# Products by C in the selective scan: five on VectorE with states left in PSUM, eleven on GpSimd

## The reference

```
xn    = rmsnorm(x) * norm_w
xp, z = split(xn @ Win)                       # 256 channels each
xc    = silu(causal_conv4(xp) + conv_b)
dt, B, C = split(xc @ Wx)                     # 64, 16, 16
delta = softplus(dt @ Wdt + bdt)
h[t]  = exp(delta[t] * A) * h[t-1] + (delta[t] * xc[t]) * B[t]     # 256 channels x 16 states
y[t]  = sum over states of h[t] * C[t]  +  xc[t] * Dp
x     = x + (y * silu(z)) @ Wblk
```

## Time and profile before

| | us |
|---|---|
| timed runs, median of 3 (lowest, highest) | 2146.39 (2145.01, 2146.58) |
| profiled execution, span from first to last instruction | 2143.5 |

### The profile page before, as it was taken

The page is one execution under the profiler, slowest core; times in us unless marked ns, Lnnn a source line. Parts: engine busy times, 40 slices in busy tenths (PEclk is TensorE's granted clock), DMA queues, the critical chain, the costliest instruction groups (busy, mean ns, idle before and its releaser), DMA issues.

```text
span 2143.5 us, 34659 instructions
## 1 busy us (share of the span) xinstructions
PE 1877.8 (88%) x10816; PEld 1183.1 (55%) x10816; DVE 1943.2 (91%) x1826; ACT 1683.8 (79%) x3053; POOL 1458.1 (68%) x1364
## 2 busy tenths in 40 slices
PE   4788888888888888888888888888888799999998
PEld 1444444444444444444444445444444499989998
DVE  3799999999999999999999999999999987767775
ACT  4899999899999998989999999999999433333333
POOL 2688888888888888888888988888889600000000
PEclk9899999999999999999999999999999999999999
DMA  7323232323232323232333333332322200000000
GB/s 241 86 64 79 63 78 62 78 62 78 62 79 63 80 65 79 64 79 65 81 78 73 81 76 79 78 78 62 78 62 72 84 1 11 11 12 11 11 6 11
DMA packets 72786, 138.55 MB, mean 65 GB/s; under 512 B 13072, under 2 KB 31120, under 8 KB 68112
## 3 DMA queue, kind: packets, MB, share of 16 engines
q1 hardware_dynamic: 66320, 119.28, 22.7%
q10 hardware_dynamic: 6400, 18.42, 3.7%
HBM read 63.85 MB, written 7.74 MB: 33 GB/s over the span
## 4 chain that ended last, share of the span: by engine, by line
ACT 27%; PE 26%; POOL 26%; issue 13%; DVE 6%; ACTq 1%; SPq 1%; DMA 1%; POOLq 0%; DVEq 0%
POOL scan L478 12%; POOL scan L472 11%; PE y_ps L1291 11%; ACT decay L563 10%; PE dbu_ps L1266 8%; ACT scan L641 6%; DVE scan L829 3%; POOL scan L469 2%; PE dbu_ps L1067 2%; ACT sp_e L600 2%; ACT delta L601 2%; ACT sp_l L610 2%; PE y_ps L1052 2%; ACT sp_e L605 1%; ACT du_t L626 1%
## 5 line engine op out<-in xcount | busy, mean ns | idle before, releaser
L829 DVE TENSOR_TENSOR_SCAN scan<-decay,dbu_ps 128x1024 f32<-128x1024 f32 x512 | 1154.6, 2274 | 29.8 <-PE dbu_ps L1067 21.9
L1067 PE MATMUL dbu_ps<-ident,scan 128*128 128x128 f32 x4096 | 571.6, 286 | 220.7 <-DVE scan L829 195.9
L478 POOL TENSOR_TENSOR scan<-scan,c_rep 128x1024 f32<-128x1024 f32 x255 | 671.8, 2635 | 130.4 <-ACT du_t L626 66.5
L1067 PEld LDWEIGHTS dbu_ps<-ident,scan 128*128 128x128 f32 x4096 | 482.2, 147 | 500.1 <-DVE scan L829 259.3
L563 ACT ACTIVATE decay<-d_rep,a_cur 128x510 f32<-128x510 f32 x1024 | 668.0, 709 | 54.1 <-POOL scan L478 15.7
L472 POOL TENSOR_SCALAR scan<-du_t,b_t 128x256 f32<-128x256 f32 x896 | 594.8, 679 | 0.0
L641 ACT ACTIVATE scan<-du_t,b_t 128x256 f32<-128x256 f32 x1024 | 445.6, 494 | 1.2
L838 DVE TENSOR_TENSOR scan<-scan,c_rep 128x1024 f32<-128x1024 f32 x257 | 331.0, 1288 | 0.0
L766 ACT ACTIVATE decay<-dbu_ps 128x512 f32<-128x512 f32 x256 | 147.9, 597 | 205.2 <-PE dbu_ps L1266 183.1
L1052 PE MATMUL y_ps<-scan,sel 128*32 128x512 f32 x2048 | 299.8, 661 | 0.0
L1080 PE MATMUL pre_ps<-xn,w_pre 128*128 128x512 f32 x512 | 245.5, 603 | 5.2 <-DVE w_pre L818 5.2
(11 more groups left out here) (110 smaller groups left out, 1648.8 us busy)
## 6 DMA issues: line engine op xcount, KB each, us to landing
d_rep<-delta SPq DMA_DIRECT2D x496, 128.0 KB, 2.9
c_rep<-c_rows SPq DMA_DIRECT2D x32, 1024.0 KB
w_pre<-prepared_weights ACTq DMA_DIRECT2D x15, 866.0 KB, 13.0
prepared_weights<-scan SPq DMA_DIRECT2D x3, 1122.0 KB, 12.9
scan<-in_conv_w SPq DMA_DIRECT2D x4, 512.0 KB, 5.0
w_out<-prepared_weights SPq DMA_DIRECT2D x16, 128.0 KB, 12.5
sp_e<-in_x_rows SPq DMA_DIRECT2D x8, 256.0 KB, 3.2
d_rep<-in_w ACTq DMA_DIRECT2D x2, 1024.0 KB, 6.8
```

The costliest lines, as they stand in the source:

```text
L478: nc.gpsimd.tensor_tensor(ring[slot % RING], ring[slot % RING], c_rep[par][:, slot // PRS, :].unsqueeze(1).broadcast_to([128, 2, TG]), ALU ...
L829: nc.vector.tensor_tensor_scan(ring[slot % RING].rearrange("p u t -> p (u t)"), decay[slot % DEC].rearrange("p u a t -> p (u a t)"), dbu_p ...
L1067: last = nc.tensor.transpose(dbu_ps[slot % 2][:, u, 128 * j:128 * j + 128], dbu_t[m % 2][:, j, b, :, :].rearrange("p q c -> p (q c)"), ide ...
```

## The change

Six things are changed together.

1. Five of a step's 16 products by C (slots 0, 4, 8, 12, 14) are made on DVE and eleven on POOL; before it was eight and eight. In the five slots the scan writes its states back into `dbu_ps`, and the product reads them there and writes the `ring`. The product follows its own scan directly (before, it followed the next slot's scan). PE may refill that `dbu_ps` tile only when the product is done.
2. The bias bdt becomes row 96 of the weights of `project_dt`, and a row of ones is added to `dbc`. The Relu parts of softplus go from ACT; the two Abs become one of 1024 elements over both banks; DVE's last sum reads max(dt, 0) straight from PSUM.
3. `silus` is cut in two: x in slot 3 ahead of that slot's `outer`, z in slot 4 behind that slot's `exps`.
4. `turn_b` and `copy_bt` come ahead of `project_dt` (slots 5 and 6), whose two matmuls now wait for `root` (slot 7); Abs, Exp, Square and Ln follow each other in slot 8.
5. `project_out` uses the bank `y_ps[1]`, in slot 8, and `copy_out` follows the logarithm in slot 8; the second `skip` matmul waits for that copy.
6. Conv taps, `quad`, `turn_du`, `outer` shares and `normalise` move by a slot or so; an `outer` share that is empty no longer waits.

The diff, cut to its core:

```diff
+DVE_SLOTS = (0, 4, 8, 12, 14)
-SHARE = (0, 2, 5, 8)
+SHARE = (0, 3, 5, 8)
-POOL_SHARE = (0, 2, 3, 4, 4)
-POOL_FIRST = (0, 0, 2, 3, 4)
+POOL_SHARE = (0, 2, 2, 4, 4)
+POOL_FIRST = (0, 1, 3, 4, 4)
+UPPER_TAPS = (0, 3, 4)
+LOWER_TAPS = (0, 1, 3, 4)
 ...
+                sp.dma_start(pre[l][NBC:NBC + 1, W_DT:W_DT + DI].rearrange("a (k p) -> a k p", k=KT),
+                             bdt[l:l + 1, :, :].rearrange("a p k -> a k p"),
 ...
             def outer(s, par, m, first, last):
-                if first == 0:
+                if first == 0 and last:
 ...
-            def softplus_parts(s):
-                    nc.scalar.activation(sp_e[:, k, :], bank, ACT.Abs, bias=bias)
-                    nc.scalar.activation(delta[:, k, :], bank, ACT.Relu, bias=bias).then_inc(dt_used, 1)
+            def softplus_abs(s):
+                act.wait_ge(dt_ready, 2 * s + 2)
+                nc.scalar.activation(sp_e[:, :, :], pre_all[:, :, :], ACT.Abs).then_inc(act_sp, 1)
+                act.wait_ge(act_sp, 2 * s + 1)
+                nc.scalar.activation(sp_e[:, :, :], sp_e[:, :, :], ACT.Exp, scale=-1.0).then_inc(act_sp, 1)
 ...
+                    if slot == 3 and has(s, 1):
+                        silu_x(s + 1, nxt)
                     if has(s, 0) and m < M and p:
                         outer(s, par, m, SHARE[p - 1], SHARE[p])
-                    if slot == 3 and has(s, 1):
-                        silus(s + 1, nxt)
+                    if slot == 4 and has(s, 1):
+                        silu_z(s + 1)
 ...
             def scan(s, slot):
+                states = dbu_ps[slot % 2][:, :, :] if by_vector(s, slot) else ring[slot % RING]
-                nc.vector.tensor_tensor_scan(ring[slot % RING].rearrange("p u t -> p (u t)"),
+                nc.vector.tensor_tensor_scan(states.rearrange("p u t -> p (u t)"),
 ...
-                nc.vector.tensor_tensor(ring[slot % RING], ring[slot % RING],
+                nc.vector.tensor_tensor(ring[slot % RING], dbu_ps[slot % 2][:, :, :],
 ...
-                            nc.vector.tensor_tensor(delta[:, :, :], delta[:, :, :], sp_l[:, :, :], ALU.add)\
+                            nc.vector.scalar_tensor_tensor(out=delta[:, :, :], in0=pre_all[:, :, :], scalar=0.0,
+                                                           in1=sp_l[:, :, :], op0=ALU.max, op1=ALU.add)\
 ...
-            def project_dt(s):
-                pe.wait_ge(dbc_ready, s + 1)
+            def project_dt(s, k):
+                if k == 0:
+                    pe.wait_ge(bt_ready, s + 1)
+                elif has(s, 1):
+                    pe.wait_ge(ln_done, s + 2)
```

More of the change, by code:

```diff
@@ L58 @@
 W_CB = W_DT + DI
-W_DB = W_CB + KT
-W_D = W_DB + KT
+W_D = W_CB + KT
 W_PRE = W_D + DI
@@ L304, in is_last, with by_vector, vector_products, pool_products @@
             return has(s, 0) and not has(s, 1)
+        def by_vector(s, slot):
+            return slot in DVE_SLOTS or is_last(s) and slot == SLOTS - 1
+        def vector_products(s, slot):
+            return DVE_C * s + sum(by_vector(s, n) for n in range(slot + 1))
+        def pool_products(s, slot):
+            return POOL_C * s + sum(not by_vector(s, n) for n in range(slot + 1))
         def has(s, offset):
@@ L1062, in to_channels @@
                     pe.wait_ge(dbut_act, ACT_OUTER * (M * s + m + 1))
-                wait(pe, scan_done, SLOTS * s + slot - 1)
+                back, before = (s, slot - 2) if slot >= 2 else (s - 1, slot - 2 + SLOTS)
+                if has(s, -1) or slot >= 2:
+                    if by_vector(back, before):
+                        pe.wait_ge(hc_dve, vector_products(back, before))
+                    else:
+                        pe.wait_ge(scan_done, SLOTS * back + before + 1)
                 for u in range(2):
@@ L1138, in turn_du @@
                 pe.wait_ge(du_ready, s + 1)
-                pe.wait_ge(bt_ready, s + 1)
-                wait(pe, x_ready, s - 1 + X0 if has(s, -2) else 0)
                 for h in range(2):
@@ new lines, in window @@
+                    if slot == 5 and has(s, 1):
+                        turn_b(s + 1)
+                    if slot == 7 and has(s, 1):
+                        project_dt(s + 1, 1)
+                        project_dt(s + 1, 0)
+                    if slot == 8 and has(s, 0):
+                        skip(s, i, par, 1)
+                    if slot == 6 and has(s, 0):
+                        quad(s, 0, 0)
+                    if slot == 9 and has(s, 0):
+                        quad(s, 0, 1)
+                    if slot >= 9 and slot % 2 and has(s, 0):
+                        quad(s, (slot - 5) // PRS, (slot - 5) % PRS // 2)
```

176 lines of the change are left out of this document (83 added, 93 removed).

## The result

The changed kernel takes 2169.6 us (median of 2164.7 to 2186.4), the kernel before took 2145.7 beside it: ratio 1.0141, 95% interval 1.0114 to 1.0167. It is slower, where 2136 and "faster" were forecast. The profiled execution is the fastest of the four: 2164.69 us, span 2162.9.

The account below looks back on a forecast made before the run. ACT was taken to lead, DVE following closely. ACT's terms sum to -0.28 us per window (51.2), -8.4 over some 30; with -4 and +1.5 at the ends, span 2132.6, plus 2.9 for the median: 2136 us, range 2106 to 2174.

Parts of the forecast that it names:

- terms 1 to 3: ACT per window: z wait goes -2.29, dbc wait -0.24; softplus with one Abs -1.19; two more table loads +2.84 us.
- The start: Passed once: new dt wait and `turn_b` ahead of dt about +1, bdt loads +0.5 us.
- Term 4: ACT at the Abs: new wait for dt, which now follows `root`, +0.45 us per window if PE stands ready.
- term 5: ACT's wait for the DMA of delta into `d_rep`, now paid in full: 0 to 0.33, taken +0.15 us per window.
- Term 2: ACT's softplus: one Abs of 1024 elements handing over to Exp replaces four parts, -1.19 us per window.
- the relief of products: POOL's products fall from 2.635 towards the undisturbed 2.36 us; eight give 2.2 us back per window.
- the tail's -4: Last window, where ACT waits for DVE: fewer DVE products save 5 us, taken as -4.
- Of the rivals the second: Hand-overs between ACT and PE from dbc copy to Abs replace the z wait; slower, about 2167 us; chance 0.27.

Follow-up runs that it names:

- e9: Kernel before the change, with one more wait on SP so the load of C is issued later in each window: 2148.3 us, ratio 1.0035.
- e2: Changed kernel with the reload of `w_pre` cut to the bias columns, so that part of the work is left out: 2141.4 us, ratio 0.9991.
- e7: Changed kernel with the copy of dbc, and so the store and load of C, moved to slot 4 straight behind the z silus: 2159.4 us, ratio 1.0084.
- e1: Changed kernel with POOL's normalisation moved back from slot 6 to slot 7, behind the product of slot 6: 2154.8 us, ratio 1.0061.
- e10: Changed kernel with the edits of e1 and e2 together, normalisation later and no full reload of `w_pre`: 2109.1 us, ratio 0.9843.
- e8: Changed kernel with z silus behind slot 3's copies, C's copy in slot 4, reload ahead of Abs, normalisation later: 2114.5 us, ratio 0.9858.

## Why the prediction was wrong

**What held.** ACT's terms 1 to 3 came nearly as priced: the z and dbc waits are gone, and ACT is busy 48.6 us per window (1118.40 in 23.0), where the terms make 47.3 - 1.19 + 2.84 = 49.0. ACT's table loads, answering to the earlier trace rows:

```profile
798.02 1.29 ACT L658 ACTIVATE scan<-du_t,b_t 128x256 f32<-128x256 f32 x3
799.33 1.28 ACT L583 ACT_TABLE_LOAD   x1
800.63 1.33 ACT L583 ACTIVATE decay<-d_rep,a_cur 128x510 f32<-128x510 f32 x2
801.98 1.28 ACT L601 ACT_TABLE_LOAD   x1
803.27 1.08 ACT L601 ACTIVATE sz<-pre_ps 128x512 f32 x2
```

It is 1.31 us from end to start at a load, with no drain. A scan into PSUM (second row, 2277 ns in the mean) costs what one into SBUF does:

```profile
L850 DVE TENSOR_TENSOR_SCAN scan<-decay,dbu_ps 128x1024 f32<-128x1024 f32 x351 | 789.7, 2274 | 29.5 <-PE dbu_ps L1094 20.1
L850 DVE TENSOR_TENSOR_SCAN dbu_ps<-decay,dbu_ps 128x1024 f32<-128x1024 f32 x161 | 366.6, 2277 | 86.4 <-PE dbu_ps L1094 86.3
```

POOL's products take 2367 ns. POOL was relieved by more than assumed, 44.3 us per window instead of 49, as its `outer` products fell too, from 679 to 480 ns. The undisturbed windows, 50.6 to 51.1, come near the forecast's 51.2, though DVE's softplus is held in them too. The start cost +1.5, as said; its two parts were not measured apart. Term 4 was 0.19 instead of 0.45.

**What failed: term 5**, "paid in full: between 0 and 0.33, I take +0.15". ACT's wait for the broadcast rose from 0.33 to 1.04 us per window (23.9 / 23.0), +0.71. Its bound was wrong, since it took the landing as fixed. It rightly said that such a wait is now paid in full: in the kernel before, a window with a wait of 3.2 us takes 53.1 where its neighbours take 51.5, as its z wait is 1.0 instead of 2.55; in the changed kernel one with a wait of 5.0 takes 55.7 where the undisturbed ones of its kind take 50.6. But the landing moved, by 2.3 us. Term 2's own gain (1.19 us) brings the logarithm, and the reload behind it, nearer to the load of C: C's store lay 13.29 us ahead of the logarithm's end and lies 12.06 ahead. e9 makes most of this shift alone, 1.0 us, and the landing follows by 1.6; e2 and e7 show that it goes with how the three transfers lie. The remaining 0.7 us are within the scatter of the means. delta's 2 us have no share that e1 could show.

**What had no term: the softplus on DVE.** The prediction saw that POOL and DVE disturb each other and credited the relief of products. It took DVE's softplus to stay as it was, three instructions in 3.8 us, without a row for the new order. It did not ask which instructions with two SBUF inputs remain on DVE and what POOL now issues beside them. The first of the three took, before and after (min/median/max ns):

```profile
L860 DVE SCALAR_TENSOR_TENSOR sp_w<-sp_w,sp_e x32: 1204/1240/1480, 38.3 to 1632.7; 128x1024 f32<-128x1024 f32 x32
L882 DVE SCALAR_TENSOR_TENSOR sp_w<-sp_w,sp_e x32: 1224/3385/3406, 39.7 to 1651.6; 128x1024 f32<-128x1024 f32 x32
```

It is over 3 us in 29 of 32 windows. By e10 against e2 this costs 32 us, 1.04 per window, where no broadcast wait is in the way, partly as the wait for the turned du (0.66 per window, 0.06 before); with the reload in place e1 gets back 15.

Of this du wait a part comes with PE's clock. The window of 774.6 us, with a du wait of 1.8, shows it:

```profile
770.00:775.00 5.00, 3.94 (x33) 2.07 (x31) 4.93 (x4) 5.00 (x12) 1.32 (x2) 1.00 0.31 90
775.00:780.00 5.00, 3.22 (x16) 1.73 (x16) 5.00 (x3) 4.38 (x9) 5.00 (x6) 0.69 0.80 176
```

All windows of 400 to 1600 us with a du wait above 1 us have a stretch at 1.2 GHz that begins 1.2 to 3.7 us behind du, and those without one wait 0.34 at most. e1, with the softplus free, has next to no such wait (0.2 us in all). What the clock does to it was not tried by itself. The kernel before has such a stretch behind nearly every du as well, without the wait.

By terms: -0.26 (term 4), +0.56 (term 5), +0.60 (du), and +0.28 for ACT waiting for a scan of DVE make +1.18 per window over the forecast, and 0.97 was measured; ACT's own work, 0.3 to 0.4 below the sum, covers the difference. With both losses gone e10 lies 0.95 below the forecast's window for the same reasons: ACT's work (0.3), the Abs (0.26), and the broadcast, for which the sum still held 0.48 and e10 shows 0.09. Of the tail's -4 came 2.4: the last interval is that much shorter, and behind it nothing changed. Of the rivals the second was nearest, by its sign and its time of 2167; but the time is right by chance, as its place was wrong: the Abs and the dbc copy, where it saw the wait, wait 0.19 and 0 us.

## What to carry to other kernels

When a wait goes, ask what it has been paying for: here it absorbed late transfers, and without it each microsecond of lateness counts in full. Whoever shortens work between two DMA issues moves the transfers together, so draw all large transfers of a period on one time line before bounding any wait for them. And when work moves between two engines that hold each other up, as DVE and POOL do here, list every instruction with two SBUF inputs that is left, with what the other engine starts just ahead of it, not only those that moved.

## What the runs showed of the hardware

A DVE operation with two SBUF inputs that came 0.04 us behind a POOL product lasted 3.40 us; with that product out of its way (e1) it lasts 1.22. A scan of 1024 elements that writes to PSUM takes 2277 ns, one that writes to SBUF 2274. A change of ACT's tables took 1.31 us from the end of the instruction ahead to the start of the next.

Three transfers, 3.9 MB in all, run at one time here, and the landing of the last goes with the other two: without the second (e2) it moved from 18.6 to 13.4 us, with the first issued 3.1 us earlier (e7) from 18.6 to 13.4, and with the first 1.0 us later (e9) from 16.3 to 17.9. In a wait of PE of 2.55 us (e8) the granted clock went to 1.2 GHz, and dt took 3.78 us instead of 1.96.
